# A four-layer gated model on one core: rows prepared in other steps of the second attention, and the second expert stage adding into the output

## The reference

```python
x = x + tanh(g_xattn[0]) * L0_xattn(ctx, layernorm(x), mask, ...)        # 8 heads of 64, keys: 120 ctx rows + 512 rows of x
x = x + tanh(g_ffn[0])   * L0_ffn(layernorm(x), scores, expert_weights, expert_indices, w1, w2, bias)
x = x + tanh(g_xattn[1]) * L1_xattn(layernorm(x), ctx, wq, bq, wk, ...)  # 16 heads of 32, keys: 120 ctx rows
x = x + tanh(g_ffn[1])   * L1_ffn(layernorm(x), gate_w, w1, w2, w3)

def L1_ffn(x, gate_w, w1, w2, w3):          # 8 experts, the best 2 of each token
    scores = softmax(x @ gate_w.T)
    top_scores, sel = top_k(scores, 2)
    # token t, choice c, expert e = sel[t, c]:
    y = (silu(x @ w1[e]) * (x @ w3[e])) @ w2[e]      # D = 512, H = 1024
    out[t] += y * top_scores[t, c]
```

## Time and profile before

| | us |
|---|---|
| median of 3 runs (lowest, highest) | 4455.71 (4453.83, 4456.92) |
| the profiled execution | 4459.2 |
| its span, first to last instruction | 4457.5 |
| PE busy in the span | 4043.5 (91%) |
| DVE, ACT, POOL busy | 2940.7 (66%), 1962.1 (44%), 846.1 (19%) |
| HBM read, written | 543.15 MB, 57.67 MB |

### The profile page before, as it was taken

One profiled execution on the slowest core, in us unless ns is written; L12 is line 12 of the kernel. 1 busy time (PEld: TensorE's weight loads), 2 busy tenths in 40 slices (PEclk: granted clock), 3 DMA queues, 4 the chain that ended last, 5 costly groups with the idle time before them and its releaser, 6 DMA issues. The chain is left out here.

```text
span 4457.5 us, 67316 instructions
## 1 busy us (share of the span) xinstructions
PE 4043.5 (91%) x23584; PEld 3134.5 (70%) x23584; DVE 2940.7 (66%) x4503; ACT 1962.1 (44%) x2732; POOL 846.1 (19%) x878
## 2 busy tenths in 40 slices
PE   5999999998589999999987998949999999999991
PEld 2444444544379999999964555549999999999990
DVE  2555656656467667676725777658777777777774
ACT  2555555554144444444523444414444444444440
POOL 2111112210101101011113655401111111111106
PEclk9999999998789999999998999959999999999995
DMA  2000000000165656555630111026666666666648
GB/s 78 21 12 29 28 28 28 12 17 20 55 221 205 209 206 207 208 205 204 210 137 3 60 59 43 28 72 222 207 210 212 216 209 207 210 213 217 207 165 306
DMA packets 377789, 602.41 MB, mean 135 GB/s; under 512 B 19464, under 2 KB 180296, under 8 KB 377672
## 3 DMA queue, kind: packets, MB, share of 16 engines
q1 hardware_dynamic: 338600, 502.31, 32.8%
q0 software_dynamic: 17600, 57.69, 3.9%
q10 hardware_dynamic: 21472, 40.90, 2.5%
HBM read 543.15 MB, written 57.67 MB: 135 GB/s over the span
## 5 line engine op out<-in xcount | busy, mean ns | idle before, releaser
L974 DVE TENSOR_TENSOR e_WL<-e_raw,e_WH 128x2048 fp32r<-128x2048 f32 x418 | 957.5, 2291 | 469.9 <-ACT e_WH L934 461.4
L896 PE MATMUL bank<-e_xh,e_WH 128*128 128x256 f32 x3968 | 1126.5, 284 | 39.9 <-ACT e_hf L950 20.1
L934 ACT ACTIVATE e_WH<-e_raw 128x2048 fp32r<-128x2048 f32 x418 | 799.1, 1912 | 799.7 <-PE bank L912 574.7
L896 PE MATMUL bank<-e_xl,e_WH 128*128 128x256 f32 x3968 | 1126.2, 284 | 0.0
L896 PE MATMUL bank<-e_xh,e_WL 128*128 128x256 f32 x3968 | 1125.9, 284 | 0.0
L896 PEld LDWEIGHTS bank<-e_xh,e_WH 128*128 128x128 f32 x3968 | 765.1, 193 | 43.4 <-issue 29.5
L896 PEld LDWEIGHTS bank<-e_xl,e_WH 128*128 128x128 f32 x3968 | 765.0, 193 | 2.3
L896 PEld LDWEIGHTS bank<-e_xh,e_WL 128*128 128x128 f32 x3968 | 765.0, 193 | 0.0
L912 PE MATMUL bank<-e_WH,e_hh 128*128 128x512 f32 x1360 | 534.9, 393 | 0.0
L912 PE MATMUL bank<-e_WH,e_hl 128*128 128x512 f32 x1360 | 529.7, 389 | 0.0
L912 PE MATMUL bank<-e_WL,e_hh 128*128 128x512 f32 x1360 | 529.0, 389 | 0.0
(11 more groups left out here) (197 smaller groups left out, 5621.8 us busy)
## 6 DMA issues: line engine op xcount, KB each, us to landing
e_raw<-in_w SPq DMA_DIRECT2D x262, 1024.0 KB, 5.4
e_raw<-in_w SPq DMA_DIRECT2D x312, 512.0 KB, 4.3
y<-e_Yo ACTq DMA_DIRECT2D x62, 512.0 KB, 3.0
a_X<-in_x SPq DMA_DIRECT2D x32, 256.0 KB, 2.6
a_R<-in_x SPq DMA_DIRECT2D x32, 256.0 KB, 3.8
x<-a_R SPq DMA_DIRECT2D x32, 256.0 KB, 2.0
a_X<-x SPq DMA_DIRECT2D x32, 256.0 KB, 3.2
x<-a_X SPq DMA_DIRECT2D x32, 256.0 KB, 2.0
```

The source lines that it names most:

```text
L896: mm = nc.tensor.matmul(up[n % RING][:, q * ROWS:q * ROWS + ROWS], w, x[:, c, :], start=(c == 0 and i == 0), stop=(c == DC - 1 and i == 2))
L934: act.activation(WH[:, p, :], raw[:, s, :], ACT.Copy).then_inc(high_ready.sem, 1)
L974: dve.tensor_tensor(WL[:, p, :], raw[:, p % 2, :], WH[:, p, :].bitcast(F32), ALU.subtract)\
```

## The change

Two parts.

*Second attention.* The helpers `bias`, `add`, `root` and `norm` are called at other steps, by four small tables (step: (which batch ahead, block)). The transposition `yt` of block 3 moves from step 2 to step 3 on PE and ACT. `load_x` is called for `n+3` after the stores of a body instead of for `n+2` before them. Each finished row block is stored twice, to `x3` and to the output.

*Second expert stage.* There is no `combine` and no `y1`. The router writes its probabilities times the gate (4096 rows of 8 numbers) to a DRAM tensor `share`. Per tile POOL gathers, besides the rows, each row's 8 numbers by two more indirect DMAs; DVE picks the number of the tile's expert by a one-hot product and a sum (`wnext`, copied to `wcol`); ACT scales the result by it on the way out of the banks; POOL then adds the 256 scaled rows into the output by two indirect DMAs with an addition at the destination, and waits for their landing. POOL's loop is turned: root of tile `j+1`, fetch of tile `j+2`, scatter of tile `j`. Empty slots point to 256 spare rows behind the output, behind `x3` and behind `share`, which `setup` zeroes by six DMAs.

```diff
@@ setup @@
+            pool.memset(spare[:, :], 0.0).then_inc(blank, 1)
...
+                sp.wait_ge(blank, 1)
+                for r in range(NTOK, SPARED, P):
+                    sp.dma_start(k.x3[r:r + P, :], spare[:, :]).then_inc(spared, 16)
+                    sp.dma_start(k.out[r:r + P, :], spare[:, :]).then_inc(spared, 16)
+                    sp.dma_start(k.share[r:r + P, :], spare[:, 0:E]).then_inc(spared, 16)
+                sp.wait_ge(spared, 48 * ROWS // P)
...
@@ route_top2 @@
+                dve.tensor_scalar(part[:, :, :], pr[:, :, :], k.gate[:, 3:4], None, ALU.mult).then_inc(shared, 1)
...
-                then(dve.tensor_scalar(k.w1[:, :], top[:, :], k.gate[:, 3:4], None, ALU.mult))
+            @block.sync
+            def _(sp):
+                sp.wait_ge(shared, 1)
+                sp.dma_start(k.share[0:NTOK, :].rearrange("(t p) e -> p t e", p=P), part[:, :, :]).then_inc(stored, 16)
+                sp.wait_ge(stored, 16)
...
@@ experts, POOL @@
                     for m in range(MT):
                         pool.indirect_dma_start(X[:, m, :], None, src, bass.IndirectOffsetOnAxis(icol[:, m:m + 1], 0))\
                             .then_inc(x_in[m], 16)
+                    if gated:
+                        for m in range(MT):
+                            pool.indirect_dma_start(prow[:, m, :], None, k.share, bass.IndirectOffsetOnAxis(icol[:, m:m + 1], 0))\
+                                .then_inc(p_in, 16)
...
+                def scatter(j):
+                    pool.tensor_copy(ocol[:, :], idx_i[:, ds(j * MT, MT)]).then_inc(ocopied.sem, 1)
+                    pool.wait_ge(ocopied.sem, ocopied.have(j, 0))
+                    pool.nop(nofuse=True)
+                    pool.wait_ge(y_ready.sem, y_ready.have(j, MT - 1))
+                    pool.nop(nofuse=True)
+                    for m in range(MT):
+                        pool.indirect_dma_start(k.out, bass.IndirectOffsetOnAxis(ocol[:, m:m + 1], 0), Yo[:, m, :], None,
+                                                compute_op=ALU.add, oob_is_err=True).then_inc(y_out, 16)
+                    pool.wait_ge(y_out, j * 32 + 32)
+                    pool.nop(nofuse=True)
+                    pool.sem_inc(landed, 1)
+                if gated:
+                    pool.sem_inc(landed, 1)
+                    fetch(0)
+                    root(0)
+                    fetch(1)
+                    with pool.Fori(0, nt - 2) as j:
+                        root(j + 1)
+                        fetch(j + 2)
+                        scatter(j)
...
@@ experts, ACT @@
+                        act.wait_ge(landed, j + 1)
+                        act.nop(nofuse=True)
+                        act.wait_ge(wcol_ready, j + 1)
+                        act.nop(nofuse=True)
+                        act.wait_ge(down_done.sem, down_done.have(j, DOWN - 1))
+                        for m in range(MT):
+                            act.activation(Yo[:, m, :], down[m], ACT.Copy, scale=wcol[:, m:m + 1]).then_inc(y_ready.sem, 1)
...
@@ experts, DVE, in norm behind the two bn_stats @@
+                    if gated:
+                        dve.wait_ge(p_in, j * 32 + 32)
+                        dve.tensor_tensor(pick[:, :, :], prow[:, :, :], k.te1_hot[:, ds(j, 1), :].to_broadcast([P, MT, E]), ALU.mult)\
+                            .then_inc(picked, 1)
+                        dve.wait_ge(picked, j + 1)
+                        dve.tensor_reduce(wnext[:, :], pick[:, :, :], AX.X, ALU.add).then_inc(wnext_ready, 1)
...
@@ attention1 @@
-          (("pv", 2), ("yt", 1), ("pv", 3), ("yt", 2), ("yt", 3)),
-          (("o", 0), ("q", 0)),
+          (("pv", 2), ("yt", 1), ("pv", 3), ("yt", 2)),
+          (("yt", 3), ("o", 0), ("q", 0)),
...
+BIAS1_AT = {0: (2, 0), 1: (2, 1), 5: (2, 2), 6: (2, 3)}
+ADD_AT = {1: (2, 0), 2: (2, 1), 7: (2, 2), 0: (1, 3)}
+ROOT1_AT = {2: (2, 0), 3: (2, 1), 0: (1, 2), 1: (1, 3)}
+NORM1_AT = {3: (2, 0), 4: (2, 1), 1: (1, 2), 2: (1, 3)}
...
-def combine(nc, k, out):
```

More of the change, by code:

```diff
@@ L598, in route @@
         one_na = sb("one_na", [P, na])
+        tok, empty = (sb("tok", [P, B * QT]), sb("empty", [P, nh])) if te_hot is not None else (k.tokcol, None)
+        spare = sb("spare", [P, nh])
         pre_b, tot_b = k.bank[:, 0, 0:E * na], k.bank[:, 1, 0:E * na]
@@ L683, in _ @@
                 dve.wait_ge(used, na)
-                then(dve.tensor_copy(idx_i, inv_b))
+                if te_hot is None:
+                    then(dve.tensor_copy(idx_i, inv_b))
+                else:
+                    then(dve.scalar_tensor_tensor(empty[:, :], inv_b, 0.0, spare[:, :], ALU.is_equal, ALU.mult))
+                    then(dve.scalar_tensor_tensor(idx_i, inv_b, float(NTOK), empty[:, :], ALU.add, ALU.add))
 def route_given(nc, k, ins):
@@ L721, in route_top2 @@
         step, expd = sem("step"), sem("expd")
-        centred = sem("centred")
+        centred, shared, stored = sem("centred"), sem("shared"), sem("stored")
+        part = sb("part", [P, NT, E])
         wide = lambda v: v.unsqueeze(2).to_broadcast([P, NT, E])
@@ L806, in experts @@
         raw_round = UP // 2 * raw_step + DOWN // 2 * 16
-        icopied = count("icopied", 1)
+        icopied, ocopied = count("icopied", 1), count("ocopied", 1)
+        landed = sem("landed")
+        p_in, picked, wnext_ready, wcol_ready = sem("p_in"), sem("picked"), sem("wnext_ready"), sem("wcol_ready")
         stepped, stat, rst = count("bn_step", MT), count("stat", MT), count("rstd_ready", 1)
@@ L851, in _, with fetch @@
             def _(pool):
-                def gather(j):
+                def fetch(j):
                     pool.wait_ge(x_read.sem, x_read.back(j, MT - 1, MT))
@@ L864, in gather @@
                     pool.tensor_tensor(rstd[:, :], veps[:, :], k.halfneg[:, 0:MT], ALU.pow).then_inc(rst.sem, 1)
-                with pool.Fori(0, nt) as j:
-                    gather(j)
+                def scatter(j):
[19 more added lines that the diff above has]
+                        scatter(j)
+                    root(nt - 1)
+                    scatter(nt - 2)
+                    scatter(nt - 1)
+                else:
+                    with pool.Fori(0, nt) as j:
+                        fetch(j)
+                        root(j)
             @block.tensor
@@ L963, in _ @@
                 tiles(act, body)
-                act.wait_ge(y_out, 16 * (nt + 1))
+                if not gated:
+                    act.wait_ge(y_out, 16 * (nt + 1))
             @block.vector
@@ L1154, in _ @@
                 for n in bodies:
-                    if -1 <= n < B - 2:
-                        load_x(n + 2)
                     if 0 <= n - 1 < B:
@@ L1219, in _ @@
                             root3(n - 1, NORM3_AT[s])
-                        if 0 <= n + 2 < B:
-                            if 3 <= s < 3 + QT:
-                                root(n + 2, s - 3)
-                            if s < QT:
-                                bias(n + 2, s)
+                        if s in ROOT1_AT and 0 <= n + ROOT1_AT[s][0] < B:
+                            root(n + ROOT1_AT[s][0], ROOT1_AT[s][1])
+                        if s in BIAS1_AT and 0 <= n + BIAS1_AT[s][0] < B:
+                            bias(n + BIAS1_AT[s][0], BIAS1_AT[s][1])
                         if softmax(n):
@@ L1388, in _ @@
                             keep_turned(u, 0)
-                        if rest[0][0] == "pv":
+                        short = rest[0][0] in ("pv", "yt")
+                        if short:
                             empty(n, rest.pop(0))
@@ L1392, in _ @@
                             exp(STEPS1 * n + s)
-                        if s != 2:
+                        if not short:
                             empty(n, rest.pop(0))
@@ L1581, in build @@
         route_top2(nc, k)
-        experts(nc, k, "e1_", k.x3, ins["w1_1"], ins["w3_1"], ins["w2_1"], FF1, NT1, k.idx1, k.te1, k.y1)
-        combine(nc, k, out)
+        experts(nc, k, "e1_", k.x3, ins["w1_1"], ins["w3_1"], ins["w2_1"], FF1, NT1, k.idx1, k.te1, None)
 def kernel(**inputs):
```

110 lines of the change are left out of this document (43 added, 67 removed).

## The result

The changed kernel takes 4357.38 us, median of 4 runs (4354.49 to 4360.36), beside 4456.32 (4453.83 to 4456.97) for the kernel before on the same chip: a ratio of 0.9779, 95% interval 0.9762 to 0.9796. The forecast was 4345, the range 4322 to 4375. The profiled execution took 4355.28 us, its span 4353.5. The total is 12 us off, but one term behind it is 15 us off, others miss by some us the other way, and one bound was wrong.

What follows compares the result with a forecast made beforehand. PE bounds the expert stages; four attention bodies lose about 9 us each to waits, and the combine runs 100.1 us without PE. Terms sum to -110.8: 4459.2 to 4348.4, less 3.5 for the median, forecast 4345, range 4322 to 4375.

Steps and rivals of the forecast that it cites:

- The combine goes: Kernel's end: 100.1 us without PE replaced by evictions and two adding DMAs, landing taken as 7 us: -90.3 us (-92 to -82).
- The second attention: Four bodies with gathered rows fall to 59 us each as PE's waits for `a_gated` go: -30, body before them -1.
- The 2 us a body: Second attention, DVE steps 0 to 2: two adds per body meeting a POOL instruction, 1.76 instead of 0.74 us each.
- DVE keeps the bound: Rival, second attention: blocked adds and normalizations in steps 0 to 2, 62 to 63 us a body, 4361; chance 0.20.
- The steady tile: Second experts: tile stays at PE's 34.80 us, the adding DMAs' landing hidden: 0 us (0 to +8).
- bound 16: Second experts' tile: landing up to 11 us costs nothing, PE is delayed only beyond a landing near 16 us.
- the addition lands too late: Rival, second experts: landing beyond 16 us delays root, `scale` and PE's transpositions; 4497 at 20 us; chance 0.05.
- Router: Router: DVE's extra products +1 us, exposed store of `share` in 32-byte pieces +5 us; together +6.
- start: Start of second experts: first statistics also wait for the two gathers of `share`: +2.5 us (+1 to +4).
- The rival on small pieces: Router and setup: store of `share` exposed for 16 to 20 us, and setup's stores too: 4359; chance 0.12.
- Setup: Before the barrier: six more DMAs and a landing delay the first load by +2 us (0 to +5).

Runs made afterwards that it cites:

- bias early: Changed kernel with POOL's bias (addition and two gathers) of blocks 2 and 3 in steps 2 and 3 instead of 5 and 6: 4332.28 us, ratio 0.9719.
- rows early: Changed kernel with only POOL's two gathers for blocks 2 and 3 moved to steps 2 and 3, bias addition staying in 5 and 6: 4331.62 us.
- sum early: Changed kernel with only POOL's bias addition for blocks 2 and 3 moved to steps 2 and 3, the two gathers staying in 5 and 6: 4347.81 us.

## Why the prediction was right, and where it was not

*The combine goes: -90.3, measured -87.5.* The step held. ACT's eviction started when it should; the second adding DMA started 2.6 us behind `Yo`'s end, not 1.7, because POOL's start takes 0.8 us behind it and the issue is 1.55 us long; and it took 8.7 us to the end of the span where I took 7, within the bounds of 5.7 to 15.6. Reading and writing does not double a landing: 7.0 against 5.3 in the loop.

*The second attention: -31, measured -16.3.* The mechanism I named (adds out of the steps in which `result` is due, so that ACT gets its buffer) is what shortens the bodies, and bias early shows its full size: 57.0 to 57.3 a body, -37 for the four. In the changed kernel the four gave 11.6 of the 30 us forecast; the body before them gave 3.0 instead of 1. What failed is the sentence that POOL's full steps 5 and 6 cost nothing because the share is used two steps later. That asks only who waits for POOL's results. It does not ask which DVE instruction stands beside POOL's, although the prediction used this very hold for the adds, from the earlier trace rows. I moved it to steps 0 to 2, where POOL has gaps and the adds take 0.74 to 0.85 us, and looked at none of the steps into which POOL's own instructions move. The 2 us a body was right in kind, wrong in place, and too small: the bodies stand 6.5 us above the floor (254.30 / 4 = 63.6 against 57.1), 4.6 us above the 59 forecast. The rival *DVE keeps the bound* gave the size (62 to 63 a body, gain 15) and had the wrong place: with the same adds in steps 0 to 2 and the bias early there is nothing left of it.

The Trainium skill (SBUF — State Buffer, section Who interferes with whom) says that a DVE instruction with two inputs in SBUF contends with a GpSimd instruction that reads SBUF, that one with at most one does not outside the two-port modes, and that who issues first has the shared pair. The trace agrees on the inputs for this addition (0.71 us with one in the bank, 3.87 and 4.21 with two in SBUF). On the order it agrees in rows early (0.65 us in a gap of 0.65, and then POOL's share 2.14 instead of 1.8), but not in the changed kernel: there `result` starts 0.30 and 0.62 us before POOL's residual by the profile and is held. A hold through one whole instruction, as I had taken the rule, would have been 1.8 to 2.5 us by my estimate; DVE was held through two, and in step 6 of sum early through one (0.80). The measurement decides: a price for one hold is no bound.

*The steady tile: 0, measured 0.* 34.80 us in both kernels, with a landing of 7.0 as taken. The room behind it was overstated, bound 16, measured 11.5 to 12.3. So the case *the addition lands too late* would have needed a landing of some 14 us instead of 19: the whole gain of 99 us is 2.6 us a tile. It was still far off.

*Router +6, measured +1.0; start +2.5, measured +1.2.* DVE's extra instructions are the 1.0. The store of `share` was issued at 2896.3 and landed 4.5 us later, within DVE's chain: nothing of it is exposed. The nearest row I took, a load of 512 pieces whose issue took 1.23 us, said nothing of a store's pieces: this one has 4096 and its issue is 0.38 us. The rival on small pieces is refuted for this store. What the rule on pieces below 512 bytes that the prediction took from the Trainium skill (DMA: Bandwidth & Descriptors, Specifications) costs isn't told by this run, since nothing waited for it; it doesn't make 128 KB in 4096 pieces take more than 4.5 us.

*Setup: +2, measured +2.6.* As taken: six issues from 1.72 to 4.57, a landing, then the barrier.

The forecast's 12 us are then: attention +14.7 and the end +2.8 too optimistic, router and start 6.3 too dear, setup and tiles +1.1, the untouched stretch -5.4, and the profiled run stood 2.1 us below the median instead of 3.5 above, 5.6. They come to +12.5. That the total is only 12 us off is luck: errors of both signs met. That it lies in the range is not, since the errors that made the forecast too short, taken alone, come to 24 us and would have given 4369; but the range reached that high for the case *DVE keeps the bound*, not for the hold that was there.

## What to carry to other kernels

When instructions are moved on one engine, list what stands beside them on the engine that shares its memory port, in the step they leave and in the step they enter, and for both engines' instructions; a hold found in one place (1.76 instead of 0.74) is to be reckoned with wherever such a pair meets, and it can be dearer there (4.21 instead of 0.69). Ask not how busy POOL is in the step but whether it has a gap at the moment when DVE's two-operand instruction is due: a wait of POOL for DVE's previous instruction is such a gap and is worth keeping. Without a gap the outcome could change from one body to the next (0.65 or 4.2 us), so a time that rests on it is not a safe one. And a slack read from a trace holds only as long as what starts the clock (here `Yo`) is not itself moved by the delay.

## What the runs showed of the hardware

- A DVE addition of two SBUF operands was held through two successive POOL instructions (3.06, 3.87 and 4.21 us instead of 0.69), each time ending 0.55 or 0.56 us behind the end of the second. By its recorded start it had begun up to 0.62 us before the first of the two. The change from one POOL instruction to the next let it in in step 6 of sum early (0.80 us, in four bodies of four) and not in step 5 (3.06); a wait of POOL of 0.65 us let it in each time.
- POOL's indirect DMA issues did not hold it: in the kernel with only the second experts changed a `result` beside a gather (2592.02, the gather from 2591.97 to 2592.92) took 0.68 us.
- An indirect DMA of 256 KB that adds at its destination is issued in 1.55 to 1.9 us and lands in 7.0 (median), one that overwrites in 0.96 to 1.3 and 5.3; the row gathers of 256 KB in the expert stages landed in 7.1 and the gathers of 32-byte rows in 4.8. In the second attention, at a DMA share of 0.21 to 0.27, gathers of 256 KB landed in 3.5, so a landing is a price of its stretch and not of the DMA alone.
- The granted clock goes with these waits: 0.95 to 0.97 in the bodies with a wait of 3.96 us, 1.00 in the same bodies once it is gone, with PE's busy time falling from 58.2 to 55.6 us. Of the 6.3 us that a body gained in bias early 2.6 are slower matmuls, not waiting.
